# A group's running sum is kept in PSUM instead of SBUF while its gathered experts are added

## The reference, cut to what matters

```python
x = x + attention(layernorm(x), ctx, Wq, Wk, Wv, Wo)        # residual, called y below
xt = layernorm(x).reshape(-1, 256)
shared = einsum('tse,she->th', gelu(einsum('th,seh->tse', xt, shared_up)), shared_down)
probs = softmax(xt @ router_w.T)
topk_p, topk_i = top_k(probs, 4)                            # the gate of each chosen expert
routed = sum over the 4 chosen experts e: topk_p[e] * (gelu(xt @ up[e].T) @ down[e].T)
out = x + shared + routed
```

## Time and profile before

| what | value |
|---|---|
| median of 3 runs | 3096.67 us (3094.06 to 3101.54) |
| profiled execution, its own time | 3078.89 us |
| its span | 3077.1 us |
| busy share of the span: PE, DVE, ACT, POOL | 72%, 55%, 32%, 60% |
| share of the last chain: PE, POOL, DVE, issue | 39%, 20%, 17%, 9% |
| granted TensorE clock, mean | 0.851 |
| DMA, mean over the span | 137 GB/s |

### The profile page before, as it was taken

How to read it: one execution, slowest core, us unless ns; L and a number is a source line. 1 busy time by engine, 2 the same in 40 slices (tenths; PEclk the granted TensorE clock), 3 DMA queues, 4 the chain that set the end, 5 groups by cost and what they waited for, 6 DMA issues and landing times.

```text
span 3077.1 us, 55896 instructions
## 1 busy us (share of the span) xinstructions
PE 2219.2 (72%) x21056; PEld 1713.7 (56%) x21056; DVE 1683.0 (55%) x4681; ACT 974.5 (32%) x1826; POOL 1843.3 (60%) x1716
## 2 busy tenths in 40 slices
PE   6888888888888888888886299999994333334331
PEld 3655556556565656655654288888894233323321
DVE  3555555554555555545554288888873544454444
ACT  2433333333333333433332155555551010101100
POOL 2355555545555555555544566666657777777776
PEclk8999988888889999999996599999997666666665
DMA  4223232222222232222222377777784555455543
GB/s 171 67 71 104 73 98 72 89 86 87 87 74 94 70 98 79 92 83 83 83 73 69 123 277 274 275 276 276 275 296 147 154 164 156 149 159 160 154 128 119
DMA packets 207370, 420.50 MB, mean 137 GB/s; under 512 B 25601, under 2 KB 124929, under 8 KB 207106
## 3 DMA queue, kind: packets, MB, share of 16 engines
q1 hardware_dynamic: 157954, 282.65, 27.5%
q0 software_dynamic: 49152, 134.28, 13.4%
HBM read 215.50 MB, written 201.33 MB: 135 GB/s over the span
## 4 chain that ended last, share of the span: by engine, by line
PE 39%; POOL 20%; DVE 17%; issue 9%; another core or an unknown queue 9%; ACT 6%; DMA 1%; POOLq 0%; DVEq 0%; SPq 0%; ACTq 0%
POOL gb L1004 19%; PE A L382 5%; PE A L355 5%; PE A L433 4%; PE A L450 4%; PE A L549 4%; PE A L533 3%; ACT pr L593 3%; PE A L472 3%; DVE mx L682 3%; PE A L437 3%; DVE xl L866 3%; PE A L516 3%; PE A L465 2%
## 5 line engine op out<-in xcount | busy, mean ns | idle before, releaser
L967 POOL DMA_INDIRECT xs<-xn,idx x512 | 502.1, 981 | 695.5 <-PE A L450 305.5
L1004 POOL DMA_INDIRECT gb<-ys,idx x512 | 587.6, 1148 | 174.3 <-issue 174.3
L516 PE MATMUL A<-ident,xr 128*128 128x128 f32 x1408 | 209.7, 298 | 472.7 <-DVE xl L866 421.4
L516 PEld LDWEIGHTS A<-ident,xr 128*128 128x128 f32 x1408 | 180.2, 154 | 512.8 <-issue 446.0
L593 ACT ACTIVATE pr<-A 128x512 f32<-128x512 f32 x512 | 264.4, 603 | 551.7 <-PE A L437 280.6
L900 DVE SCALAR_TENSOR_TENSOR ob<-gb,gw,ob 128x256 f32<-128x256 f32 x512 | 205.6, 479 | 416.3 <-DMA gb<-ys,idx 404.0
L682 DVE TENSOR_REDUCE mx<-A 128x4 f32<-128x512 f32 x512 | 316.7, 680 | 178.3 <-remote 125.8
L615 ACT ACTIVATE xh<-A 128x512 fp32r<-128x512 f32 x352 | 194.0, 599 | 365.9 <-PE A L516 198.6
L621 ACT ACTIVATE act<-A 128x512 f32<-128x512 f32 x208 | 124.2, 598 | 528.3 <-PE A L533 261.9
L989 POOL TENSOR_TENSOR hl<-act,hh 128x512 fp32r<-128x512 f32 x144 | 187.2, 1300 | 146.8 <-DVE hh L871 146.8
L549 PE MATMUL A<-wt,hh 128*128 128x256 f32 x1152 | 241.7, 293 | 0.0
(11 more groups left out here) (158 smaller groups left out, 4616.8 us busy)
## 6 DMA issues: line engine op xcount, KB each, us to landing
xr<-xs SPq DMA_DIRECT2D x144, 512.0 KB
ys<-yo SPq DMA_DIRECT2D x144, 512.0 KB, 3.9
xb<-in_x SPq DMA_DIRECT2D x32, 512.0 KB
cg<-in_ctx_t SPq DMA_DIRECT2D x32, 512.0 KB
yd<-xb SPq DMA_DIRECT2D x32, 512.0 KB, 3.1
x2d<-xn SPq DMA_DIRECT2D x32, 512.0 KB, 3.3
xr<-x2d SPq DMA_DIRECT2D x32, 512.0 KB
yr<-yd SPq DMA_DIRECT2D x32, 512.0 KB
```

The source lines that it names most:

```text
L516: ins = tr(banks[c][:, q * P:(q + 1) * P], xr[t % 3][:, q, c * P:(c + 1) * P], ident[:, :])
L967: q.indirect_dma_start(xs, bass.IndirectOffsetOnAxis(ap=idx[:, n, k:k + 1], axis=0), x2[g % 4][:, i, :], None).then_inc(sent[g % 4], 16)
L1004: q.indirect_dma_start(gb[p][:, i, k, :], None, ys, bass.IndirectOffsetOnAxis(ap=idx[:, n, k:k + 1], axis=0)).then_inc(got[p], 16)
```

## The change

The 16 additions of a group keep their running sum in the two PSUM banks of the shared product. The residual is added in place, into the bank. The additions of the first three experts (k = 0, 1, 2) read the sum from the bank and write it there; those of the fourth read the bank and write the tile `ob[p]` in SBUF. So before, an addition of line 900 has the inputs `gb` and `ob`, both in SBUF, and its output in SBUF; after, it has `gb` in SBUF and the bank in PSUM as inputs, and its output is in PSUM twelve times of sixteen. The gate `gw` stays in SBUF.

The banks are released by the last addition that reads them, and no longer by the addition of the residual. Per group, `add_done` now counts 2 + 12 + 2, and the two `drain` counts of the banks stand for the last additions of each bank: SP's store and POOL's gather(g + 2) wait for all three.

```diff
@@ SP, SUM(g)
-                sp.wait_ge(add_done, TOPK * GT * (g + 1))
+                sp.wait_ge(add_done, 16 * (g + 1))
+                for b in FFN_BANKS["DN"](NT + g):
+                    wait_drained(sp, b, "DN", NT + g)
@@ DVE, SUM(g)
-                for k, b in enumerate(FFN_BANKS["DN"](NT + g)):
+                own = FFN_BANKS["DN"](NT + g)
+                def part(i):
+                    return banks[own[i // 2]][:, (i % 2) * E:(i % 2 + 1) * E]
+                for k, b in enumerate(own):
                     wait_filled(dve, b, "DN", NT + g)
-                    v.tensor_tensor(ob[p][:, 2 * k:2 * k + 2, :].rearrange("p q e -> p (q e)"), banks[b][:, :],
-                                    yr[p][:, 2 * k:2 * k + 2, :].rearrange("p q e -> p (q e)"), ALU.add).then_inc(drain[b], 1)
-                for b in FFN_BANKS["DN"](NT + g):
-                    wait_drained(dve, b, "DN", NT + g)
-                dve.wait_ge(got[p], 16 * GT * TOPK * (g // 2 + 1))
+                    v.tensor_tensor(banks[b][:, :], banks[b][:, :], yr[p][:, 2 * k:2 * k + 2, :].rearrange("p q e -> p (q e)"),
+                                    ALU.add).then_inc(add_done, 1)
                 for k in range(TOPK):
+                    dve.wait_ge(got[p], 16 * GT * TOPK * (g // 2 + 1))
                     for i in range(GT):
-                        if k > 0:
-                            dve.wait_ge(add_done, (TOPK * g + k - 1) * GT + i + 1)
-                        ins = v.scalar_tensor_tensor(ob[p][:, i, :], gb[p][:, i, k, :], gw[:, g * GT + i, k:k + 1],
-                                                     ob[p][:, i, :], ALU.mult, ALU.add).then_inc(add_done, 1)
+                        before = i // 2 if k == 0 else 2 + (k - 1) * GT + i
+                        dve.wait_ge(add_done, 16 * g + before + 1)
+                        out_ = part(i) if k < TOPK - 1 else ob[p][:, i, :]
+                        ins = v.scalar_tensor_tensor(out_, gb[p][:, i, k, :], gw[:, g * GT + i, k:k + 1], part(i),
+                                                     ALU.mult, ALU.add)
+                        if k == TOPK - 1 and i % 2 == 1:
+                            ins.then_inc(drain[own[i // 2]], 1)
+                        else:
+                            ins.then_inc(add_done, 1)
@@ POOL, gather(g)
-                wait(pool, add_done, TOPK * GT * (g - 1))
+                if g >= 2:
+                    pool.wait_ge(add_done, 16 * (g - 1))
+                    for b in FFN_BANKS["DN"](NT + g - 2):
+                        wait_drained(pool, b, "DN", NT + g - 2)
```

## The result

The changed kernel takes 3152.45 us (3150.09 to 3154.35, 4 runs) against 3099.11 us of the kernel before on the same chip: a ratio of 1.0168, with a 95% interval of 1.0141 to 1.0195. The forecast was 3001 us and its range ended at 3050. A second pair of runs, on another chip, gave 1.0167 [1.0145, 1.0188].

What follows compares the result with a forecast made beforehand. The prediction took POOL's issuing of 512 gathers to bound the last stage. Hold gone, -106 us, plus 10 for CASTs gave -96, so 3096.7 - 96 = 3001 us, range 2985 to 3050.

Steps and rivals of the forecast that it cites:

- The loss that I saw: Last stage: bursts of DVE additions with two SBUF inputs hold POOL's gathers up, 3.4 us per burst; taken as gone.
- Rival A: Additions hold gathers by their kind of instruction, not their inputs; every group keeps its 3.4 us: 3097 us, 17%.
- rival C: Slower: the hold stays and additions in PSUM or their waits lengthen the burst, holding gathers longer: 3122 us, 7%.
- Rival B: Part of the hold is in the output; four additions still writing `ob` in SBUF keep 26 us: 3027 us, 12%.
- The size: Total loss from held gathers in the last stage, over 31 bursts of additions: 106 us, all taken off.
- The CASTs: DVE's two `hh<-act` behind each burst still hold gathers, 0.34 us in 30 groups: 10 us, bounds 0 to 26.
- PSUM as output: DVE additions writing PSUM take as long as before, 479 ns; no difference, bounds -0.9 to +3.6 us at the end.
- Banks held longer: The two banks are released about 20 us later, but PE's next write already waits behind the last addition: cost 0.
- The two added waits of POOL: Extra waits before a group's first gather, 30 times: taken as 0, 18 us at a whole pause each.
- What comes next: After the change: POOL stays the bound at 20.2 us per group, transfers fit, DVE keeps some 8 us of pause.
- PSUM as an output of DVE: Its slack argument: a burst need only end by the first gather of the group after next, 15.3 us later.
- A POOL row that waits for DVE: Sign of a wrong forecast in the last stage: POOL waiting for DVE would mean the slack was misread.

Runs made afterwards that it cites:

- two_sbuf_in: The changed kernel, with each group's first 12 additions taking their second input from `yr` in SBUF instead of the bank; 3142.5 us, ratio 1.0152 to the kernel before.
- narrow: The kernel before, with each addition covering only 8 of the 256 columns, so that the burst is too short to hold a gather; ratio 1.0016.
- pause3: The changed kernel, with three unused elementwise copies on POOL behind the 8th gather of each group but the first; 3094.5 us, ratio 0.9995 to the kernel before.

## Why the prediction was wrong, step by step

*The loss that I saw was real, and went.* I had forecast gathers at a mean of 970 to 990 ns, none over 1.6 us, and groups of 20.2 to 20.9 us: measured were 965 ns, at most 1.21 us, and 20.2 to 20.5 for most groups between the stalls. Rival A is refuted by the gathers and by two_sbuf_in, rival C by both. Rival B falls with POOL's rows beside the four additions that write `ob`, which in the changed kernel run from 2358.42 to 2360.07:

```profile
2358.61 0.96 POOL L1018 DMA_INDIRECT gb<-ys,idx  x1 [0.30 <-issue]
2359.87 0.96 POOL L1018 DMA_INDIRECT gb<-ys,idx  x1 [0.30 <-issue]
2361.13 1.16 POOL L1018 DMA_INDIRECT gb<-ys,idx  x1 [0.30 <-issue]
```

Both beside them take 0.96 us; the 1.16 us is beside the CAST and the subtractions behind. The Trainium skill, SBUF — State Buffer, section "Who interferes with whom", says that a DVE instruction with at most one input in SBUF, outside the two-port modes, does not contend; the 1.21 us maximum agrees. The same section infers of `tensor_tensor` with two SBUF inputs that it leaves descriptor generation alone. The lone subtraction `hl<-act,hh` agrees with that (0.96 us); the row of `scalar_tensor_tensor` with two such inputs does not: 3.59 us before, 1.67 and 2.46 in two_sbuf_in.

*The size was a little off.* I read the 2.37 us pause of the earlier trace rows as additions that begin in a pause. But four pauses of this length stand after the change too, 2.11, 2.32, 2.40 and 2.11 us, with no addition near them that has two inputs in SBUF. They stand before the 114th, 226th, 338th and 450th gather, seven groups apart, in every kernel here with 512 gathers (only narrow has one of 0.62 us among its four).

```profile
2683.57 0.96 POOL L1018 DMA_INDIRECT gb<-ys,idx  x1 [2.32 <-issue]
```

They are POOL's own, some 8 us of the 106 I took off. The hold was worth about 98 us.

*The CASTs* were put at 10 us. Measured: five gathers over 1.1 us, together 1.1 us above 0.96 each, and 4 us over all 512 gathers against the old median of 957 ns. The 0.34 us that I had read off the end of a held gather does not carry over to one that nothing holds.

*PSUM as output:* 481 and 473 ns against 479, a burst of 6.35 us against 6.42. Taken as 0, was 0. *Banks held longer:* taken as 0; the table of waits has no wait of PE on the additions of line 907, and narrow stalls with the banks released early. *The two added waits of POOL:* the pause is 0.30 us as before wherever DVE is in time.

*The step that failed is "What comes next":* "POOL stays the bound, by its 1.26 us per gather". I checked that the transfers fit (180 GB/s) and that DVE had pause to spare. The 8 us that I gave it does not come out of my own rows (404 / 31 is 13.0, less 3.2 for the shorter group is 9.8; where nothing is late, DVE waits 9.66 us for its rows, at 2374.25), but either is enough. Both checks were taken from averages of a state that the change removes. I took PE's and DVE's pace as given. It was not: it rested on the 3.4 us per group in which a gather was held up. The slack argument under "PSUM as an output of DVE", "15.3 us later", is sound only if the burst comes when it did. With the hold gone, POOL runs at full pace for three groups, PE falls to one instruction in 1.40 us, DVE waits up to 31.1 us for the shared product (173.0 us in all), and POOL waits in turn: -98 from the hold, +154.5 from ten waits, +1 from the rest, is +57 us. The last sentence of the prediction's signs, "A POOL row that waits for DVE would mean that I misread the slack", is the one that came true.

Could the trace of before have told it? Only in part. It has no slow piece and no wait of POOL. What the profile of before did show is that the hold was the one break that every group of POOL's gathers had. I named no rival in which that break did something for others, and rival C, my slower case, was tied to a longer hold.

*What stays open.* The runs show that gathers without a break starve PE and DVE, that 3 us per group prevent it and 1 us does not, and that the demand of the engines matters. They don't show what is shared. Instruction supply is one candidate; the recording of each instruction for the profile is another, as the timed runs carry that record too. The trace of after speaks against the first in its plainest form, a PE that has run out of instructions. The queue of instruction transfers brings 172 blocks of 16 KB in a run, one for about 256 of PE's 44098 records, so they are most likely PE's. None begins between 2336.8 and 2434.8 us. Yet PE runs 108 matmuls and weight loads at full pace from 2422.5 us on, before the block at 2434.8. If the trace has all blocks, these had been loaded long before, and so had the slow ones ahead of them. And in the later stretches the slow pace begins anywhere from 61 to 248 records behind the last block, but always 17 to 20 us behind POOL's restart. I tried no version with the gathers issued on another engine.

No kernel here beats the kernel before with its work complete: pause3, at 0.9995, is the same. Removing the hold and putting a rest in its place is an exchange of like for like.

## What to carry to other kernels

A stall that shows in every period may be somebody else's break: before taking it away, list who makes progress in it, and predict the case in which they lose it. When the engine that sets the pace gets faster, don't take the others' slack from the old averages; test it cheaply first, by a run that makes the pace-setter faster by leaving work out, as narrow does. And look for pauses named "issue" of equal length: a table of waits lists them without a releaser (PE's line 551 after the change: 244.7 us in 135 pauses; none of that line before), and only the timeline shows that they are all alike.

## What the runs showed of the hardware

- While POOL issues indirect DMAs back to back, 0.96 us each and 0.30 us apart, PE falls to one instruction in 1.40 us (weight load and matmul each count), first after 70 us, and after a stop of some 15 us again within 17 to 20 us; it is back at full pace 1 to 9 us after POOL stops (all in the changed kernel). DVE shows the same distance between its two additions at 2380.72 and 2382.15. Of PE's slow pieces and POOL's waits, a break of about 3 us per group leaves none; 2.2 us leave 230 of 357 and 47.8 of 155.7 us, 1.2 us leave 280 and 91.3 us. An elementwise copy on POOL counts as a break.
- Sixteen additions on end with both tensor inputs in SBUF hold an indirect DMA until 1.17 us behind their end (0.83 where no CAST follows), 2.41 to 5.18 us by where it starts in them; twelve, 1.3 to 2.5 us. With one input in PSUM no gather takes over 1.21 us, wherever the output goes.
- An addition with output in PSUM takes 481 ns, with output in SBUF 473 ns, of 128x256 f32.
- POOL has a pause of 2.1 to 2.8 us before the 114th gather and every 112 further on (some 165 us apart before the change), whatever DVE does; of 52 such pauses in the 13 profiles with 512 gathers one is shorter, 0.62 us in narrow.
